# First stage, last batch: keys, values and the last queries after the step sizes; four GpSimd products issued in the middle stage

## The reference

```
x = x + attention(layernorm(x))                 # 16 heads of 32, 2 key/value heads, causal softmax
x = x + ssm(ctx, layernorm(x))                  # z gate from x, everything else from ctx (4 x 512 x 256)
x = x + mixture_of_experts(layernorm(x))        # 16 experts, 2 per token, and a shared one

# the state-space part, per batch:
u   = silu(causal_conv4(in_proj(ctx)))          # 512 channels x 512 steps
dtl, Bm, Cm = split(x_proj(u))                  # 16 + 16 + 16 rows
dt  = softplus(dt_proj(dtl) + dt_bias)          # "step sizes"
s_t = s_(t-1) * exp(dt_t * A) + (dt_t * u_t) * B_t       # 16 states per channel, A = -exp(A_log)
y_t = sum_n s_t[n] * C_t[n] + D * u_t ;  y = y * silu(z)
```

## Time and profile before

| | us |
|---|---|
| median of three timed runs | 1238.64 (1237.73 to 1240.28) |
| the profiled execution's own time | 1238.74 |
| its span, first to last instruction | 1236.9 |
| first stage, until GpSimd's last product ends | 0 to 169.77 |
| middle stage starts | 170.11 |
| busy share of the span: PE, DVE, ACT, POOL | 87%, 65%, 54%, 54% |

### The profile page before, as it was taken

One profiled execution on the slowest core, in us unless ns is written; L12 is line 12 of the kernel. 1 busy time (PEld: TensorE's weight loads), 2 busy tenths in 40 slices (PEclk: granted clock), 3 DMA queues, 4 the chain that ended last, 5 costly groups with the idle time before them and its releaser, 6 DMA issues. The chain is left out here.

```text
span 1236.9 us, 18614 instructions
## 1 busy us (share of the span) xinstructions
PE 1073.2 (87%) x6368; PEld 642.0 (52%) x6368; DVE 806.6 (65%) x1195; ACT 668.3 (54%) x1438; POOL 673.2 (54%) x587
## 2 busy tenths in 40 slices
PE   7999838888888888888888899999999989999970
PEld 3444325555555555555555444444444457676740
DVE  5477779999999999999999476631760013333327
ACT  3566768889888888898888424202010012223220
POOL 1033369999999999999999630202041124444430
PEclk9999959999999999999999999999999999999995
DMA  6210001101111111111331212103027314333219
GB/s 204 87 36 19 18 18 35 35 28 35 35 36 32 30 35 36 36 33 63 95 102 45 90 48 103 69 34 116 20 79 244 102 44 128 127 128 129 77 49 385
DMA packets 51820, 94.74 MB, mean 77 GB/s; under 512 B 9806, under 2 KB 17998, under 8 KB 51728
## 3 DMA queue, kind: packets, MB, share of 16 engines
q1 hardware_dynamic: 44208, 72.82, 17.9%
q0 software_dynamic: 7520, 20.72, 5.4%
HBM read 74.51 MB, written 20.84 MB: 77 GB/s over the span
## 5 line engine op out<-in xcount | busy, mean ns | idle before, releaser
L604 POOL TENSOR_TENSOR w_all<-w_all 128x512 f32<-128x512 f32 x256 | 321.1, 1275 | 0.6 <-POOLq L96 0.3
L778 DVE TENSOR_TENSOR_SCAN w_all<-da,w_all 128x512 f32<-128x512 f32 x256 | 298.0, 1206 | 0.0
L712 ACT ACTIVATE da<-w_all,a_flat 128x512 f32<-128x512 f32 x256 | 179.6, 702 | 9.0 <-PEq L96 7.7
L683 PE MATMUL yb<-ident,w_all 128*128 128x128 f32 x1024 | 161.6, 281 | 7.5 <-DVE acc L786 7.5
L633 PE MATMUL sc<-w_all,attn 32*128 32x384 f32 (+3 forms) x512 | 105.0, 486 | 45.5 <-ACT w_all L720 22.8
L720 ACT ACTIVATE w_all<-sc,neg_max 128x128 f32<-128x128 f32 (+3 forms) x256 | 134.1, 539 | 16.5 <-DVE neg_max L770 15.5
L659 PE MATMUL ob<-w_all,v 128*32 128x128 f32 x1280 | 94.7, 277 | 52.8 <-ACT w_all L729 52.8
L683 PEld LDWEIGHTS yb<-ident,w_all 128*128 128x128 f32 x1024 | 113.5, 141 | 37.0 <-issue 30.6
L770 DVE TENSOR_REDUCE neg_max<-sc 128x2 f32<-128x256 f32 (+3 forms) x128 | 104.2, 814 | 34.2 <-PE sc L636 34.2
L1166 POOL TENSOR_TENSOR w_all<-w_all 128x512 f32<-128x512 f32 x24 | 29.4, 1226 | 165.0 <-ACT w_all L1337 165.0
L729 ACT ACTIVATE w_all<-tb 128x256 f32<-128x256 f32 (+2 forms) x192 | 102.8, 535 | 29.7 <-PE tb L648 29.7
(11 more groups left out here) (199 smaller groups left out, 1630.6 us busy)
## 6 DMA issues: line engine op xcount, KB each, us to landing
w_all<-b_scratch SPq DMA_DIRECT2D x64, 256.0 KB, 3.3
w_all<-in_w_up SPq DMA_DIRECT2D x16, 512.0 KB, 6.0
w_all<-in_w_down SPq DMA_DIRECT2D x16, 512.0 KB, 6.8
w_all<-sorted_y SPq DMA_DIRECT2D x16, 512.0 KB, 10.3
attn<-in_x SPq DMA_DIRECT2D x4, 1024.0 KB, 6.8
w_all<-in_x SPq DMA_DIRECT2D x16, 256.0 KB, 4.1
norms<-attn SPq DMA_DIRECT2D x4, 1024.0 KB, 4.3
out_dram<-acc SPq DMA_DIRECT2D x16, 256.0 KB, 8.9
```

The costliest lines, as they stand in the source:

```text
L604: pool.tensor_tensor(dbu[:, k, :], keep["du"][i // N][:, k * T:(k + 1) * T], b_all[i % 2][:, :], ALU.mult).then_inc(pool_dbu.sem, pool_dbu ...
L683: last = pe.transpose(yb[which][:, k * P:(k + 1) * P], state[i % 2][:, k, t * P:(t + 1) * P], ident[:, :])
L712: act.activation(da[unit % 2][:, :], keep["dt"][i // N][:, k * T:(k + 1) * T], ACT.Exp, scale=keep["a_flat"][:, unit % (N * KD):unit % (N ...
L778: dve.tensor_tensor_scan(state[i % 2][:, k, :], da[unit % 2][:, :], dbu[:, k, :], 0.0, ALU.mult, ALU.add).then_inc(dve_scan.sem, dve_scan. ...
```

## The change

All of it concerns the last batch (b = 3) except where said.

- TensorE: keys/values and query group 3 no longer stand ahead of `x_proj`. The order becomes: queries 0 to 2, `x_proj`, skip transposes, C transposes, `dt_proj`, keys/values, queries 3, value transposes. The transposed x of batch 3 goes to `w_in` and `ctx_t`, whose contents are used up by then, since the skip copies now write `acc` while queries 3 are still to be computed.
- ACT: `scale_q` of group 3 moves behind the exponentials of batch 3, ahead of the logarithms; the C copy follows the skip copies.
- VectorE: the eviction of keys and values moves behind `time_bias`, the copy of the values behind `softplus_in`.
- SP: the eight key DMAs of batch 3 follow the DMA of its B rows.
- GpSimd: the four products `du = dt * u` of batch 3 leave the first stage. The middle stage issues one after each of its first four units' products; the first `dbu` of batch 3 (unit 192 of its products) waits for them.
- A = -exp(A_log) is made in batch 1 instead of at the end of the stage.
- The semaphores of `settle` become shared by two stages.

```
+        (x_n_t of batch 3:)  (w_in if k < KC else ctx_t)[:, k % KC, :]
         # SP
-                sp.wait_ge(dve_kv.sem, dve_kv.upto(b)) ... eight DMAs
+                if b < B - 1:
+                    spread_keys(b)
                 sp.wait_ge(act_rows.sem, act_rows.upto(b))
                 sp.dma_start(d["b_rows"][b, :, :], rows[R:R + N, :])...
+                if b == B - 1:
+                    spread_keys(b)
         # GpSimd, first stage
-            weigh(B - 1)
         # TensorE
-                for m in four: ... queries
-                ... keys and values
-                ... x_proj
-            tail(B - 1)
+                for m in range(3 if b == B - 1 else 4):
+                    query(b, m)
+                if b < B - 1:
+                    key_value(b)
+                step_rows(b)
+            turn_skip(B - 1)
+            turn_c(B - 1)
+            steps(B - 1)
+            key_value(B - 1)
+            query(B - 1, 3)
+            turn_v(B - 1)
         # inside them: key_value(3) waits for dve_x.upto(12) (bank 4 read), turn_v(3) for dve_x.upto(15),
         # steps(3) for act_c (bank 7 read), turn_skip(3) for pool_skip.upto(15)
         # ACT
+                if b == 0: ... a_log = Exp(a_log)        # at the end of exponent(0)
             skip(B - 1)
+            copy_c(B - 1)
             exponent(B - 1)
+            scale_q(B - 1, 3)
             logarithm(B - 1)
-            ... a_log = Exp(a_log)
         # VectorE
-            heads_in(B - 1)
             time_bias(B - 1)
+            keys(B - 1)
             softplus_in(B - 1)
+            heads_in(B - 1)
             softplus_out(B - 1)
-            ... a_flat = -a_log
         # GpSimd, middle stage
+            def last_batch(j):
+                dt, du = [keep[n][B - 1][:, j * T:(j + 1) * T] for n in ("dt", "du")]
+                pool.tensor_tensor(du, dt, du, ALU.mult).then_inc(pool_du.sem, pool_du.tick(j))
...
                 if g + 1 < UNITS:
                     weigh(2 * g + 3)
+                if g < KD:
+                    last_batch(g)
```

More of the change, by code:

```diff
@@ L179, in load_ctx, with spread_keys @@
                 sp.dma_start(ctx_t[:, :, :], d["ctx_t"][b, :, :].rearrange("(k p) t -> p k t", p=P)).then_inc(s_c.sem, s_c.tick(b))
+            def spread_keys(b):
+                sp.wait_ge(dve_kv.sem, dve_kv.upto(b))
+                for g in range(KV):
+                    for r in four:
+                        sp.dma_start(k_4[r * DH:(r + 1) * DH, b, g, :], kv_stage[g * DH:(g + 1) * DH, :]).then_inc(s_k.sem, s_k.tick((b * KV + g) * 4 + r))
             def column(name):
@@ L296, in tail, with query, key_value, step_rows @@
                                          start=True, stop=True).then_inc(pe_dt.sem, pe_dt.tick(4 * b + j))
+            def query(b, m):
+                if b > 0:
+                    pe.wait_ge(act_du.sem, act_du.upto(4 * (b - 1) + m))
+                else:
+                    pe.wait_ge(act_xp.sem, act_xp.upto(m))
+                if b == B - 1 and m == 3:
+                    pe.wait_ge(act_du.sem, act_du.upto(4 * b + m))
+                group(bank[m][:, :], [(wq[:, k, m * P:(m + 1) * P], x_n_t(b, k)) for k in four]).then_inc(pe_q.sem, pe_q.tick(4 * b + m))
+            def key_value(b):
+                pe.wait_ge(s_kvw.sem, s_kvw.upto(3))
+                if b == B - 1:
+                    pe.wait_ge(dve_x.sem, dve_x.upto(4 * b))
+                group(bank[4][:, :], [(w_kv[:, k, :], x_n_t(b, k)) for k in four]).then_inc(pe_kv.sem, pe_kv.tick(b))
+            def step_rows(b):
+                pe.wait_ge(pool_wx.sem, pool_wx.upto(3))
+                for k in four:
+                    pe.wait_ge(act_silu.sem, act_silu.upto(4 * b + k))
+                    last = pe.matmul(bank[5][:, :], w_x4[:, k, :], u(b, k), start=(k == 0), stop=(k == 3))
+                last.then_inc(pe_rows.sem, pe_rows.tick(b))
             pe.wait_ge(s_const.sem, s_const.upto(6))
@@ L306, in _ @@
                 if b > 0:
-                    tail(b - 1)
+                    turn_v(b - 1)
+                    turn_c(b - 1)
+                    turn_skip(b - 1)
+                    steps(b - 1)
                 for k in four:
@@ L361, in exponent @@
                     act.activation(ex[:, j, :], ex[:, j, :], ACT.Exp, scale=-1.0).then_inc(act_exp.sem, act_exp.tick(4 * b + j))
+                if b == 0:
+                    act.wait_ge(s_rest.sem, s_rest.upto(6))
+                    act.activation(a_log[:, :, :], a_log[:, :, :], ACT.Exp).then_inc(act_alog.sem, act_alog.tick(0))
             def logarithm(b):
@@ L375, in _ @@
                 if b > 0:
+                    copy_c(b - 1)
                     skip(b - 1)
@@ L393, in _ @@
                 scale_q(b, 2)
-                scale_q(b, 3)
+                if b < B - 1:
+                    scale_q(b, 3)
                 if b > 0:
@@ L435, in heads_in, with keys @@
                     bank[7][:, 0:NT * KVD].rearrange("p (t g c) -> p t g c", t=NT, g=KV)).then_inc(dve_v.sem, dve_v.tick(b))
+            def keys(b):
+                dve.wait_ge(pe_kv.sem, pe_kv.upto(b))
+                if b > 0:
+                    dve.wait_ge(pe_v.sem, pe_v.upto(b - 1))
+                    dve.wait_ge(s_k.sem, s_k.upto(4 * KV * b - 1))
+                dve.tensor_scalar(kv_stage[:, :], bank[4][:, :], b_kv[:, 0:1], None, ALU.add).then_inc(dve_kv.sem, dve_kv.tick(b))
             def time_bias(b):
@@ L548, in mix @@
         dve_max, dve_scan, dve_acc, dve_rinv, dve_out = [signal("dve_" + n) for n in ("max", "scan", "acc", "rinv", "out")]
-        pool_dbu, pool_acc = [signal("pool_" + n) for n in ("dbu", "acc")]
+        pool_dbu, pool_acc, pool_du = [signal("pool_" + n) for n in ("dbu", "acc", "du")]
         s_b_all = keep["s_b_all"]
```

61 lines of the change are left out of this document (25 added, 36 removed).

## The result

| | before | after |
|---|---|---|
| median, 7 runs each | 1239.38 us (1237.44 to 1240.28) | 1234.5 us (1233.97 to 1235.84) |
| ratio after / before | | 0.9966, 95% interval 0.9954 to 0.9977 |
| span of the profiled run | 1236.9 | 1232.8 |
| first matmul of the middle stage | 170.13 | 164.57 |

The kernel became faster by 0.34%, 4.2 us (the ratio applied to the median of before; the two medians differ by 4.9). The forecast was 1236.7, 1.9 under the time before, with 1230.3 to 1239.6 as its range. In the profile of after the first stage lies about 0.48 us later than before (queries of batch 3 start at 125.83 instead of 125.35). That isn't the change: the same code reaches this place up to 1.5 us later in other executions.

What follows compares the result with a forecast made beforehand. The first stage was taken to end with one serial chain through TensorE to `time_bias`, with VectorE, ACT and TensorE closely coupled in the middle stage. 1238.74 - 3.5 (stage end) + 1.5 (middle stage) = 1236.7 us, range 1230.3 to 1239.6.

Steps and rivals of the forecast that it cites:

- `time_bias` starts (τ): First stage's end, VectorE beginning `time_bias` of batch 3: 150.8 (150.4 to 151.3), nothing gained against 150.38.
- cost in the middle stage: Start of the middle stage: Exp table load 0.9 plus VectorE's loss at product 11 0.6, together 1.5.
- the skip product loses: Batch 3's fourth GpSimd skip product is held through VectorE's eight-instruction `softplus_out` run, ends at 144.8; TensorE idles 5.4 us.
- Rival B: Fourth skip product gets in first or after one VectorE instruction, ending by 140.5; τ 144.8, time 1230.6; chance 0.20.
- rival C: Fourth skip product gets in midway through VectorE's run, at 141.8; τ 146.7 or 148.2, time 1232.6 to 1234.1; chance 0.12.
- Tail: From τ through keys/values, queries 3, Ln table and `softplus_out` to the first stage's end: 15.4 us, ending at 166.2.
- Rival E: TensorE's clock stays low through keys/values and queries 3; stage ends at 172.9, time 1243.3, slower; chance 0.07.
- The table load: ACT's Exp table load of 1.28 stands ahead of the middle stage's first decay; 0.9 of it comes through.
- the wait for product 11: Middle stage: the four moved GpSimd products make `dbu` product 11 late for its scan; VectorE loses 0.6.
- rival F: GpSimd sets the middle stage's pace and all 6.2 are paid; time 1241.4, slower; chance 0.06.

Runs made afterwards that it cites:

- the two runs on who is let in: Kernel before, one batch 3 edit each: VectorE's first `softplus_out` waits for all four logarithms, 1240.62 us; two extra ACT copies delay the logarithms, 1241.17 us.
- The run with the filled wait: Changed kernel plus seven useless 128x128 matmuls between `dt_proj` and keys/values of batch 3, filling TensorE's wait: 1233.32 us, ratio 0.9946.
- early Exp table: Changed kernel plus an Exp of one spare column at the end of ACT's first stage, loading the table there: 1235.17 us, ratio 0.9958.
- the run of the order alone: Changed kernel with the four GpSimd products of batch 3 put back at the end of the first stage: 1240.49 us, ratio 0.9996.
- the products alone: Kernel before with only the four GpSimd products of batch 3 moved to the middle stage, other order unchanged: 1235.8 us, ratio 0.9957.
- the combined kernel: Changed kernel with batch 2's `weigh` after VectorE's whole `softplus_out` run, Ln ahead of `scale_q`, Exp table loaded in first stage: 1230.77 us, ratio 0.9923.

## Why the prediction was right, and which of its steps failed

The direction and the two parts of the working, a shorter end of the first stage against a dearer start of the middle one, were right. That the sum came out within 2.2 us of the median was luck in good part: the kernel gained 4.2 where 1.9 was forecast, and the errors went both ways. The end of the stage came 2.4 earlier than forecast (the 0.48 taken off), and the middle stage's start cost 0.65 more.

| step | forecast | profile after |
|---|---|---|
| fourth skip product ends | 144.8 | 141.51 |
| clock in the transposes | 1.2 GHz | 2.4 GHz |
| `time_bias` starts (τ) | 150.8 | 147.12 |
| τ to the stage's end | 15.4 | 17.1 |
| stage ends | 166.2 | 164.25 |
| cost in the middle stage | 1.5 | 2.15 |

**The step that failed is "I take this: the skip product loses".** Its evidence was sound, but it was about a run that follows other VectorE work directly. The run in question begins behind a wait for Ln (1.78 in after), and there GpSimd is let in; the two runs on who is let in show it. The forecast had that wait in its own numbers (`softplus_out` at 139.27, `softplus_in` of batch 2 ended at 137.47) and gave it no meaning. With the product at 141.5, TensorE's wait was 1.8 instead of 5.4, and the clock stayed at 2.4 GHz through the transposes.

**Rival B was nearer on who is let in, and its τ of 144.8 failed for a reason that no rival had.** The turn-taking that lets the skip product in goes on with `weigh` of batch 2 and stretches VectorE's last four by 2.13. The τ of 146.7 of rival C is close in number only, since its skip product was to end at 142.4 and no delay by `weigh` was in it. Check: forecast start of the run 139.27, +0.47 (everything is later), +4.9, +0.42 for the third instruction, +2.13, makes 147.2; measured 147.12. The rule of the Trainium skill quoted there ("SBUF — State Buffer", section "SBUF: two separate sides") has the block, and each turn of 1.64 to 1.75 us agrees with one whole instruction waiting for the other's; which of the two outcomes applies it doesn't tell. The prediction read the trace as speaking against turns, when it spoke against them for one of two cases.

**Tail, 1.7 too short.** The list of what follows τ was right in order and, up to keys/values, in time: they start at τ + 0.9. They end at τ + 6.1 instead of τ + 4.4, since their first half ran at 1.2 GHz, and queries 3 (τ + 9.5 against 7.9), the Ln table and Ln all slide with it. Rival E had this mechanism at a chance of 0.07, with the clock falling earlier and staying low for all; in fact it fell for half a group. The run with the filled wait shows the term: without the dip the stage ends at τ + 15.6, where 15.4 was forecast. With the long dip (early Exp table) it ends at τ + 18.5.

**Middle stage, 2.15 instead of 1.5, by other terms.** The table load came through in full, 1.1 instead of 0.9, as the run with the early table shows. The moved products cost nothing in after (33.62, against 33.59 in the run of the order alone, which has none of them there): the remaining 1.0 is the clock, which was back 17 us behind the first matmul instead of 10. The two runs on who is let in show this price by themselves: their middle stage is that of before, the clock came back after 16.2 and 14.8 us instead of 9.9, and the first eight units took 32.54 and 32.44 instead of 31.48. So a late clock needs no part of the change. Whether the table load makes it likelier is not shown; all five profiles with the load at the stage's start have it, and six of the nine without. When the start of the stage speeds up, the wait for product 11 appears as forecast: 1.23 with the products alone, 0.91 with the early table, 1.24 in the combined kernel. With the clock back early it costs 0.66 in eight units, for which 0.6 was forecast. So the term was right for a kernel whose units run on time, and rival F (all of them paid) is out.

**Where the gain is from.** The prediction gave the reordering a τ with nothing gained, and 3.5 us to the shorter tail. Counted from the skip request, τ came 3.7 earlier in after (7.3 behind it instead of 11.0). That the order alone is nevertheless worth nothing (0.9996) has another reason: 2.4 of the 3.7 are lost again between τ and the middle stage, and the table load takes 1.1. On the way to the middle stage the parts add up: 30.8 before, 4.7 less with the products alone, 1.4 less with the order alone, 6.0 less with both. In the whole kernel the products alone give all of the gain (0.9957). What stays open is why the clock, once low, returned after 10 us in some executions and 15 to 17 in others, with the same middle stage too; when it dips at keys/values; and what in the chip ties the choice between holding and turns to VectorE's idle time.

## What to carry to other kernels

Where a stage ends in a serial chain, look first at what can simply leave it: here four products with cover elsewhere gave what a reordering of five engines did not. When a chain is shortened, look at who now meets whom: here it moved GpSimd's products into VectorE's run and left TensorE with waits behind which its clock fell, and a later start of GpSimd's work won more (0.9966 to 0.9931) than the new order had. A trace's case of contention holds for its conditions, so read what the engines did just before it, too. And before two profiles are compared at an absolute time, count both from one event ahead of the change, and look at when the clock came back in each: here the start of the batch alone moved by up to 1.5 us and the clock by 1.0, as much as some of the edits gave.

## What the hardware did that was not expected

- GpSimd beside a run of VectorE instructions with two SBUF inputs has two regimes. The run directly behind other VectorE work: GpSimd's product is held to the end of the run (2.85 to 2.88 us, VectorE undisturbed at 0.60 each). The run behind idle time, 0.14 us being enough: they take turns (GpSimd 1.64 to 1.71, VectorE 1.75 each).
- TensorE's clock fell to 1.2 GHz for 3.4 us although its waits before that were only 1.82, 0.76 and 2.15. With seven useless matmuls (1.83 us) in the last of these waits it didn't fall, in the one profile there is. With that wait at 0.89 it fell in one of four profiles. The dip lasted 6.8 us in two other executions with the wait of 2.15.
- The clock's return at the start of a thinly filled stage moved from 9.9 to 16.2 us behind its first matmul between executions of the same middle stage, which cost 1.0 us.
- Thirty useless matmuls that kept the clock up across a barrier lost time, 1232.9 against 1230.77: the clock then fell inside the next stage's first units and stayed at 1.2 GHz until 184.5, and the matmuls themselves ended 1.0 behind the other engines.
